# A four-layer decoder in one launch: value products divided by key tile, and sums moved between VectorE, GpSimd and TensorE

## The reference

```
scores = q @ k^T / sqrt(8)  (+ mask or bias)      # 256 x 256 for each of 16 heads and 16 sequences
out    = softmax(scores) @ v ;  y = out @ Wo + bo
block 0   self attention, rotary q and k, no mask
block 1   causal self attention plus cross attention to 64 context rows
block 3   self attention with a position bias, out * sigmoid(x @ Wg + bg)
block 6   causal (added mask) self attention, 3 times in a row with the same k and v
block 8   causal self attention, rotary (first half of a layer of its own)
block 11  last block: 16 experts, the 4 best of each row, weighted sum of their results
```

## Time and profile before

| what | value |
|---|---|
| median of 3 executions | 4092.17 us (4089.69 to 4092.91) |
| profiled execution, its own time | 4104.95 us |
| span of its records | 4103.1 us |
| PE busy | 3225.7 us (79%) |
| DVE busy | 2729.5 us (67%) |
| ACT busy | 2072.7 us (51%) |
| POOL busy | 1254.2 us (31%) |
| largest share of the chain that ended last | PE, 26% |

### The profile page before, as it was taken

The page is one execution under the profiler, slowest core; times in us unless marked ns, Lnnn a source line. Parts: engine busy times, 40 slices in busy tenths (PEclk is TensorE's granted clock), DMA queues, the critical chain, the costliest instruction groups (busy, mean ns, idle before and its releaser), DMA issues.

```text
span 4103.1 us, 91932 instructions
## 1 busy us (share of the span) xinstructions
PE 3225.7 (79%) x33262; PEld 2229.8 (54%) x33262; DVE 2729.5 (67%) x7583; ACT 2072.7 (51%) x4651; POOL 1254.2 (31%) x2347
## 2 busy tenths in 40 slices
PE   6886888696888676967898989677883579879884
PEld 2443555473556455854555555344553456669884
DVE  5884767364778576547787878476766468865455
ACT  2664656322444453535787878453660234345563
POOL 2321222102121234451111111243322424534666
PEclk9987999697999787977999999687995599989997
DMA  5423332032221322231212121423412260122323
GB/s 92 69 38 55 59 54 39 21 100 40 37 39 18 57 60 66 85 72 38 47 30 45 29 43 31 59 39 60 60 32 71 72 112 21 50 85 85 94 75 92
DMA packets 322828, 232.76 MB, mean 57 GB/s; under 512 B 53901, under 2 KB 305531, under 8 KB 322199
## 3 DMA queue, kind: packets, MB, share of 16 engines
q1 hardware_dynamic: 308106, 198.55, 24.7%
q0 software_dynamic: 13408, 27.54, 2.2%
q10 hardware_dynamic: 864, 0.79, 0.1%
HBM read 69.28 MB, written 55.75 MB: 30 GB/s over the span
## 4 chain that ended last, share of the span: by engine, by line
PE 26%; DVE 13%; POOL 7%; issue 6%; ACT 4%; DMA 2%; SPq 1%; DVEq 0%; ACTq 0%; POOLq 0%
PE ps L1505 4%; PE ps L1314 3%; PE ps L3939 2%; PE ps L3948 2%; PE ps L1348 2%; POOL PT L3763 2%; PE ps L727 2%; PE ps L1452 2%; ACT PT L1412 1%; DVE M L1362 1%; POOL L_sorted_results L3751 1%; PE ps L1126 1%; DVE X L406 1%; DMA SKB<-MT 1%; DVE BS L378 1%
## 5 line engine op out<-in xcount | busy, mean ns | idle before, releaser
L1412 ACT ACTIVATE PT<-ps 128x512 f32<-128x512 f32 (+1 forms) x1600 | 812.0, 560 | 339.6 <-PE ps L1348 247.4
L1362 DVE TENSOR_REDUCE M<-ps 128x2 f32<-128x512 f32 x1024 | 652.6, 683 | 128.6 <-PE ps L1348 103.8
L1314 PE MATMUL ps<-SKB 51*128 51x256 bf16 (+3 forms) x3584 | 414.4, 276 | 115.7 <-DVE M L1362 66.2
L1359 DVE TENSOR_REDUCE M<-ps 128x3 f32<-128x384 f32 x768 | 390.6, 550 | 150.5 <-PE ps L1348 92.7
L1505 PE MATMUL ps<-PT,VA 128*9 128x256 f32 (+1 forms) x7168 | 455.7, 374 | 1.4 <-ACT PT L1412 1.2
L4021 ACT ACTIVATE SKB<-ps,SKB 128x128 f32<-128x128 f32 x1032 | 295.1, 370 | 242.4 <-PE ps L3939 241.0
L1452 PE MATMUL ps<-SKB 53*128 53x256 bf16 (+3 forms) x3584 | 357.8, 268 | 47.2 <-DMA SKB<-MT 37.3
L1348 PE MATMUL ps<-tri,idh 64*128 64x128 bf16 x5120 | 392.9, 222 | 0.0
L4091 DVE COPY SKB<-SKB 128x1028 f32 (+1 forms) x258 | 185.7, 720 | 259.7 <-PE ps L3948 232.4
L1314 PEld LDWEIGHTS ps<-SKB 51*128 51x128 bf16 (+1 forms) x3584 | 131.2, 96 | 385.9 <-DVE M L1362 158.1
L3948 PE MATMUL ps<-SKB 128*128 128x128 f32 x2064 | 286.6, 284 | 28.4 <-ACT SKB L4021 28.3
(11 more groups left out here) (520 smaller groups left out, 6403.3 us busy)
## 6 DMA issues: line engine op xcount, KB each, us to landing
SKB<-HH SPq DMA_DIRECT2D x1212, 64.0 KB
SKB<-HH SPq DMA_DIRECT2D x576, 32.0 KB
L_sorted_results<-SKB SPq DMA_DIRECT2D x195, 64.0 KB
PT<-L_sorted_rows SPq DMA_DIRECT2D x150, 64.0 KB
SKB<-in_L3f_w SPq DMA_DIRECT2D x32, 256.0 KB, 3.6
L_sorted_rows<-TV SPq DMA_DIRECT2D x2, 4032.0 KB, 32.4
SKB<-scratch SPq DMA_DIRECT2D x2, 2048.0 KB, 11.5
SKB<-in_L1f_w SPq DMA_DIRECT2D x16, 256.0 KB, 3.2
```

Source lines behind the costliest of these rows:

```text
L1314: k = e.matmul(self.mx_bank(m + i)[:, o:o + n], K.QS[self.set(c)][64 * i:64 * i + rows, s, 256 * bb + 128 * qt:256 * bb + 128 * qt + 128], ...
L1359: k = e.tensor_reduce(K.M3[n % 2][:, hh, 0:3], mx[:, 0:384].rearrange("p (a k) -> p a k", a=3), axis=AX.X, op=ALU.max)
L1362: k = e.tensor_reduce(K.M3[n % 2][:, hh, 0:2], mx.rearrange("p (a k) -> p a k", a=2), axis=AX.X, op=ALU.max)
L1412: e.activation(K.PT[:, x % 4, n * i:n * i + n], self.st_bank(x, i)[:, 0:n], ACT.Exp, bias=0.0, scale=self.scale).then_inc(*self.exp.inc())
```

## The change

1. `pe_pv` takes a list of key tiles. For j = 0, 1, 2 tile 0 stays in slot LE+2j+3, and tile 1 moves to slot LE+2j+4, between the maxima and the scores; j = 3 keeps both in slot LE+9. V is laid out in pairs of heads, 27 columns: 8 values, a one, nine zeros, 8 values, a one. A product takes 18 of them (0 to 17 or 9 to 26), so that four calls add up in one bank: `nf` falls by one and the chain TV, transposes, normalise runs once for the self part of a unit.
2. s0, s6, s8 (`quick`): DVE normalises once, 1 reciprocal of 32 and 4 products, from PSUM. s1 and s3: ACT copies bank 7 to VN (128x288), DVE forms the reciprocals, POOL the products.
3. Maxima are stored by query tile, so that "self" maxima are negated and split with 2 instructions, not 4.
4. Offsets move: `OUT`, `TURN`, `OOS`, and the projections; V is projected 2 to 8 slots after a chunk's first start, not 13 to 19 before it, into 2 buffers, not 3.
5. s12: the roots of chunks 0 to 4 are taken on DVE; the sums of chunks 5 to 7 are identity products on PE (x and 4 results into one bank), and moments and norm read PSUM.

```
-        self.OOS = LE + (14 if cross else 12 if gate else 11)
-        self.OUT, self.TURN = self.OOS + 1, 6 if cross or gate else 5
-        self.Q, self.KP, self.V = (-30, -20, -13) if cross else (-29, -20, -19) if rope else (-29, -27, -19) if gate else (-25, -15, -19)
+        self.OOS = LE + (15 if cross else 11 if self.quick else 14)
+        self.OUT, self.TURN = (28, 5) if cross else (31, 8) if gate else (24, 8) if rope else (24, 4)
+        self.Q, self.KP, self.V = (-30, -20, 6) if cross else (-29, -20, 2) if rope else (-29, -27, 8) if gate else (-24, -13, 2)
-        self.plan(units, start, L, start[-1] + self.OUT + 12)
+        self.plan(units, start, L, start[-1] + max(36 + gate + 3 * cross, self.OUT + (10 if kind == "keep" else self.TURN) + 2))
-        self.nf, self.nm = 2 + cross, 1 + cross
+        self.nf, self.nm = 1 + cross, 1 + cross
...
+        g, half = j % 2, j // 2
+        for kt in tiles:
...
-                k = e.matmul(K.PS[32 * i:32 * i + 9, 6, 256 * g + lo:256 * g + 256],
-                             K.VA[self.set(c)][:, (2 * bb + kt) * 16 + 8 * (i % 2) + 2 * j + i // 2, :], pt[:, i % 2, o:o + 256 - lo],
-                             start=kt == 0, stop=kt == 1)
-        k.then_inc(*self.pv.inc())
+                pair = (2 * bb + kt) * 8 + 4 * (i % 2) + 2 * g + i // 2
+                k = e.matmul(K.PS[32 * i:32 * i + 18, 6, 256 * g + lo:256 * g + 256],
+                             K.VA[c % 2][:, pair, 9 * half:9 * half + 18], pt[:, i % 2, o:o + 256 - lo],
+                             start=j == 0 and kt == 0, stop=j == 3 and kt == 1)
...
+        for j in range(3):
+            u = self.at(g, LE + 2 * j + 4)
+            if u is not None:
+                self.pe_pv(e, u, j, (1,))
         if scores:
             self.pe_exp(e, *scores)
...
-                self.pe_pv(e, u, j)
+                self.pe_pv(e, u, j, (0,) if j < 3 else (0, 1))
...
+    def act_vn(self, e, f):
...
+        e.activation(self.VN, K.PS[:, 7, :].rearrange("p (x k) -> p x k", k=32)[:, :, 0:18], ACT.Copy, bias=0.0, scale=1.0
+                     ).then_inc(*self.vn.inc())
...
+    def pe_results(self, e, c):
...
+        e.matmul(total, K.idf[:, :], K.xc(c), start=True, stop=False)
...
+        for k in range(self.top):
+            o = e.matmul(total, K.idf[:, :], self.results_of(c)[:, :, k, :], start=False, stop=k == self.top - 1)
...
-        if k == top - 1 and c > 0:
-            self.tail.pool_root(e, c - 1)
...
+        if self.marked and c > 0 and k < 2:
+            (self.tail.dve_root, self.tail.dve_norm)[k](e, c - 1)
```

More of the change, by code:

```diff
@@ new lines, in dve_normalise @@
+    def dve_normalise(self, e, f, oo):
+        K = self.K
+        v = K.PS[:, 7, :].rearrange("p (q b h x) -> p q b h x", q=2, b=4, h=2)
+        r = K.RC[f % 2][:, 0:32].rearrange("p (q b h e) -> p q b h e", q=2, h=2, e=2)
+        out = oo.rearrange("p q (h d b) -> p q h b d", h=2, d=8)
+        e.wait_ge(*self.tvt.at(f))
+        sums = K.PS[:, 7, :].rearrange("p (x k) -> p x k", k=32)[:, :, 8:18:9]
+        e.reciprocal(K.RC[f % 2][:, 0:32].rearrange("p (x e) -> p x e", e=2), sums).then_inc(*K.dv.inc())
+        e.wait_ge(*K.dv.now())
+        for h in range(2):
+            for half in range(2):
+                k = e.tensor_tensor(out[:, :, h, 4 * half:4 * half + 4, :], v[:, :, :, h, 9 * half:9 * half + 8],
+                                    r[:, :, :, h, half:half + 1].to_broadcast([128, 2, 4, 8]), ALU.mult)
+        return k
@@ L1044, in __init__ @@
         self.tail.rows_in = begin and begin.rows
-        self.tail.turn_off = 9 if kind == "keep" else self.TURN
+        self.tail.turn_off = 10 if kind == "keep" else self.TURN
         self.bias = BiasSetup(K, self, W) if mode == "bias" else None
@@ L1276, in act_values @@
         self.values_free(e, c)
-        e.activation(K.VA[self.set(c)][:, :, 0:8], K.PS[:, 7, :].rearrange("p (a k) -> p a k", k=8), ACT.Copy, bias=0.0,
-                     scale=1.0).then_inc(*self.vact.inc())
+        v = K.PS[:, 7, :].rearrange("p (x e b k) -> p x e b k", e=2, b=4, k=8)
+        va = K.VA[c % 2][:, :, :].rearrange("p (x b) k -> p x b k", b=4)
+        for half in range(2):
+            k = e.activation(va[:, :, :, 18 * half:18 * half + 8], v[:, :, half, :, :], ACT.Copy, bias=0.0, scale=1.0)
+        k.then_inc(*self.vact.inc())
     def dve_values(self, e, c):
@@ L1720, in act_slot @@
             self.act_mt(e, self.nm * u)
+        for h, off in enumerate(self.TV):
+            u = self.at(g, LE + off + 1)
+            if u is not None and h < self.nf and not self.quick:
+                self.act_vn(e, self.nf * u + h)
         u = self.at(g, self.CMBT)
@@ L1799, in pool_slot @@
             self.begin.all_in(e)
+        for h, off in enumerate(self.TV):
+            u = self.at(g, LE + off + 2)
+            if u is not None and h < self.nf and not self.quick:
+                self.pool_norm(e, u, h)
         u = self.at(g, self.OOS - 1)
@@ L3959, in pe @@
                 self.pe_b2(e, c)
+        if self.marked:
+            for c in (5, 6, 7):
+                self.pe_results(e, c)
         if not self.last:
@@ L4061, in dve_sum @@
             self.tail.dve_moments(e, c)
-            if c > 0:
+            if c > 0 and not self.marked:
                 self.tail.dve_norm(e, c - 1)
```

225 lines of the change are left out of this document (135 added, 90 removed).

## The result

| | before | changed |
|---|---|---|
| median | 4091.9 us | 4102.6 us |
| ratio, 95% interval | | 1.0025 [1.0014, 1.0036] |
| profiled execution, own time | 4104.95 us | 4100.47 us |

The change makes the kernel slower by a quarter of a per cent, some 10 us; forecast was 92 us less. The two profiled executions stand the other way round, since that of before ran 12.8 us above its median; so what follows is read by stage, and the sum is left to the medians.

A forecast was written before the change was run, and what follows sets the result against it. In attention PE and DVE, both mostly near or above 80% busy, wait for each other by turns. Savings of 34 + 22 + 13 + 10 + 10.6 + 4 = 94 us from 4104.95 give 4011, as a median 3998; forecast 4000, range 3970 to 4030.

The forecast's parts named there:

- the one on the key tiles: Value products: each of three splits costs 0.13 us, 0.39 a unit; s6's unit falls from 13.1 to 12.4.
- the ends set for the unit: s6 unit: 0.19 us saved if only PE's net work counts, 1.3 if all waiting goes.
- the balance: Attention slots: each asks 1.32 us of PE and 1.28 of DVE, so the 1.0 of mutual waiting has less cause.
- the bound of 0.25: Value products: upper cost in us of each split, if both ends are paid for.
- Transposes: One of two chains leaves every unit (one of three in s1): 112 sets at 0.58, 65 us of PE.
- The ends given (-5 and 5, for V): V projected later into two buffers: nothing waits for it, taken as 0 us, ends -5 and 5.
- s0 and s8: Same edits as s6: 32 units at 0.7 us, 22 us saved.
- s1: Causal stage: 0.8 us saved a unit, 13 us in all; ends 0.2 and 1.8 a unit.
- s3: Units save 16 us, four more slots without attention give 6 back: 10 saved, ends -10 and 25.
- s12: Last stage: roots moved from POOL to DVE save 10.6 us, last sums moved to PE save 4.
- Rival C: Quick units: PE waits 1.2 us for the piled norm in each of 80; 4176 us, slower; chance 0.08.
- Rival A: Attention units: only work counts, the waits stay; 43 us saved, 4049 us; chance 0.28.

The follow-up runs named there:

- run 6: Changed kernel with the second halves of the value products behind the scores and six buffers of exponentials in s6, not four; 4069.6 us, ratio to before 0.9932.
- whole products: Changed kernel with both key tiles of a value product multiplied in the same slot, behind the scores, as before the change; 4050.6 us, ratio to before 0.9904.
- run 9: Changed kernel, whole products except in s6; there second halves behind the scores, six buffers of exponentials, K projection and stacking at old slots; 4012.2 us, ratio 0.9803.
- run 5: Changed kernel with whole products and, in s6, K projection and K stacking at their slots of before; 4026.3 us, ratio to before 0.9817.
- Run 3: Changed kernel with the K projection and K stacking of s6 at their slots of before; 4086.9 us, ratio to before 0.9982.
- run 7: Changed kernel with whole products and each set of four transposes of the values issued twice; 4075.0 us, ratio to before 0.9947.
- run 4: Kernel before with the s12 part alone (roots on DVE, last sums as PE products), attention as before; 4076.0 us, ratio 0.9964.
- run 1: Changed kernel with both key tiles of each value product in one slot behind the scores (whole products); 4050.6 us, ratio to before 0.9904.

## Why the prediction was wrong

The step that failed is the one on the key tiles, which forecast a unit of 12.4 us in s6 where 13.47 came: "a group of 16 takes 0.99 and two of 8 take 1.10, so each of three splits costs 0.11 to 0.13", and with it the ends set for the unit, 0.19 to 1.3 saved. It priced the instructions and, to the good side, the balance; it took for its worst end that "the waits as they are" would stay. It never asked what the second half stands ahead of.

- *Price of a cut.* PE's own part was too low by nearly half. Eight records take 0.56 from their start to the next instruction (2122.21 to 2122.77), as taken. But a group of products begins 0.21 after the start of the masks ahead of it (2122.00 to 2122.21), where scores begin 0.11 after it (2302.01 to 2302.12); a second group pays that 0.10 a second time: 2 x 0.56 - 0.99 + 0.10 = 0.23, near the bound of 0.25. Three cuts are 0.69 us where 0.39 was taken. The slot of 0.77 hid this: it was read with a product behind it and holds the longer entry; with none behind it a slot takes 0.67 (2301.78 to 2302.45). The slot with a half product was rightly taken at 1.32 (1.33 in run 6), the one without any too high.
- *The wait.* PE's wait for DVE in s6 fell by 31 us and the one for ACT rose by 37. Scores that come 0.65 late make exponentials 0.65 late, and the next scores need their bank. This was not in any term nor rival: PE reaching the turn of the result (rival C) was looked at, PE reaching the score banks wasn't.
- *Whether balance was there to be had.* In the regular units it was. With neither order nor buffers in the way the unit is 12.3, for the forecast's 12.4: the sum for the unit was near, its condition wrong. Over the whole kernel it brought nothing beyond whole products (run 9 against run 5), as the waits for DMA took it back.
- *Transposes.* They were counted at 0.58 each. The pairs of 3.04 and 3.19 show that one set costs 0.15 where PE waits in that slot otherwise. This fits whole products, which leave the unit at 12.87 for 13.08, though a set less and a norm less stand in it.
- *s6's DMA.* "SP's DMAs keep their order, so no shift comes to stand behind more stacking", and 0 for moving the projections. The order of issue is kept, but the K stacking moved from slots -12 to -10 to slots -11 to -9, against a period of 8 slots in which the rows of maxima have a fixed place. Run 3 puts it at 18 us by the ratios. The ends given (-5 and 5, for V) did not hold it. Nor was PE's clock a term of any attention stage, though s6 stands at its lower level for 62 us where it was 38.
- *s0 and s8.* Forecast -22, seen +6 and -2 in the traces. With whole products s0 takes 251 to 258 us in five traces and s8 216 to 217, for 259 to 261 and 223 to 225 as before: 1 to 10 and 6 to 9 saved.
- *s1.* Forecast -13, seen -4, which is not told from none; with whole products 334 to 335 us in three traces and 329 in run 9, for 342 to 349 as before, though 346.5 in run 7. *s3.* Forecast -10 out of -16 for units and +6 for slots with nothing in them; seen -16.0 (12 to 16 by the traces), and from the last turn of s3 to the next 64.2 us for 63.9. The 6 were not paid.
- *s12.* Forecast -14.6; -14.7 in run 4. No root stands among the last indirect DMAs; the sums take 21.3 us to the end (forecast 22.2), the clock reaches 1.00 about 5 us after the first sum (forecast 4).
- *Rival C* did not come: PE waited 0.6 us in all of s6 for the piled norm ahead of the turn of the result,

```profile
PE ps L821 <- DVE OO L767: 0.6, 3, 0.2
```

  so its wait of 1.2 a unit is refuted. *Rival A* (waits stay, 4049) happens to name what whole products give. The number is luck: A is priced from waits that stay because of semaphores, not of uneven slots, and run 6 speaks against this, where level slots bring PE's wait for DVE to 13.6 us from 50.8 in run 1.

The rule of the Trainium skill (TensorEngine Tiling (Array Packing), section Key Properties: a change of the tiling mode drains TensorE) was set aside for the row's 0.11 in the prediction. A cut measures 0.23, so the trace agrees with it in kind, and more of it than was taken. That a drain is what makes the 0.23 isn't shown: no run changes the tiling without a cut.

By ratios, in us: the cut +50, the K offsets +18, s12 -15, and so for the rest of the change (pairs, one chain fewer, V later, norm) -43 to reach the +10; by run 5, which has that rest and s12's part alone, it is 75 - 15 = 60 saved. The two differ by the surplus of run 5. What pairs, chain, V and norm bring one by one no run parts.

## What to carry to other kernels

When a product is cut and half of it is moved to fill an idle slot, list what stands behind it in its queue and what its operands hold: here the scores behind it and the exponentials' buffers. Levelling two engines pays only if no third one, nor a ring of buffers or banks, is tied to the old places; price that hold before pricing the instruction. An instruction taken out of a slot in which its engine waits gives back only what exceeds the wait. A transfer that is moved by one slot in a pattern with a period is a change of what it collides with.

## What the runs showed of the hardware

- Value products in four column groups begin 0.21 us after the start of a set of 4 masks, where scores begin after 0.11. Two groups of 8 apart cost 0.23 more than one of 16.
- 12 DMAs of stacking issued in a row took 8.46 us of SP's queue, and two small ones issued right behind them released PE 5.9 us after issue; with SP idle for 7 us ahead of them 3.4 us were enough (run 3).
- After 2.92 us of waiting in s6 the granted clock went from 1.00 to 0.50 and was back at 2072, 6 us on; the same PE list took 6.49 us there and 4.06 at full clock.
- A set of four transposes took 0.56 us of PE, a second one right behind it 0.44 more (run 7).
- DVE's four norms of 128 columns took 1.37 us from PSUM, 1.11 from SBUF.
- After 13.5 us of idle PE four wide products took 5.97 us, the clock at 0.50 for the first 4.5; the next four took 3.60 at 1.00.
